# Split up projection with folded gain and bias, three of sixteen products on POOL, statistics moved

## The reference

```
xz = x @ w_in.T + b_in;  x_ssm, z = split(xz);  z = silu(z)
dt = softplus(x_ssm @ w_dt.T + b_dt);  Bm, Cm = x_ssm @ w_B.T + b_B, x_ssm @ w_C.T + b_C
per token:  h = exp(A * dt) * h + dt * Bm * x_ssm      (256 channels x 16 states)
            y = sum over the states of h * Cm
y = (y + D * x_ssm) * z;  x3 = layernorm(y @ w_out.T + b_out + x) * gamma + beta
h = layernorm(x3) * ln_gamma + ln_beta
out = layernorm(x3 + 0.5 * (silu(h @ w1 + fc1_bias) @ w2 + fc2_bias))
w1 = (fc1_q - 128) * fc1_scales,  w2 the same way;   w1 is 256 x 1024
```

## Time and profile before

| | |
|---|---|
| median of 3 runs (lowest, highest) | 1116.26 us (1113.83, 1117.23) |
| the profiled execution | 1115.44 us, of it the span 1113.7 us |
| mean granted TensorE clock | 0.968 |
| PE, DVE, ACT, POOL busy | 90%, 85%, 78%, 60% of the span |
| blocks 2 to 6, from first scan to first scan | 67.0 us each |

### The profile page before, as it was taken

The page is one execution under the profiler, slowest core; times in us unless marked ns, Lnnn a source line. Parts: engine busy times, 40 slices in busy tenths (PEclk is TensorE's granted clock), DMA queues, the critical chain, the costliest instruction groups (busy, mean ns, idle before and its releaser), DMA issues. The chain is left out here.

```text
span 1113.7 us, 17417 instructions
## 1 busy us (share of the span) xinstructions
PE 1006.3 (90%) x5326; PEld 716.2 (64%) x5326; DVE 950.2 (85%) x1237; ACT 864.7 (78%) x1688; POOL 666.4 (60%) x599
## 2 busy tenths in 40 slices
PE   5999999999969999997668799999999999988987
PEld 4777777777745555555345467676676756767576
DVE  7999999999955898675899999999999899999741
ACT  7778888787646677767858898898989989896833
POOL 3456566756760123135677968788696886968320
PEclk9999999999999999999869899999999999999999
DMA  6444434442405011125987555666457664755201
GB/s 188 127 131 120 133 104 135 119 135 89 128 20 191 1 38 39 38 77 150 213 168 159 130 152 123 169 135 171 134 152 156 150 157 133 158 138 133 75 1 38
DMA packets 93233, 133.84 MB, mean 120 GB/s; under 512 B 8787, under 2 KB 47699, under 8 KB 93141
## 3 DMA queue, kind: packets, MB, share of 16 engines
q1 hardware_dynamic: 93140, 132.73, 46.3%
HBM read 116.45 MB, written 14.16 MB: 117 GB/s over the span
## 5 line engine op out<-in xcount | busy, mean ns | idle before, releaser
L2265 DVE TENSOR_TENSOR_SCAN oa<-bank_a,h,oa 128x512 f32<-128x512 f32 x128 | 159.7, 1270 | 13.1 <-ACT h L1941 10.5
L2265 DVE TENSOR_TENSOR_SCAN ob<-bank_a,h,ob 128x512 f32<-128x512 f32 x128 | 160.4, 1269 | 9.5 <-ACT bank_a L1932 6.6
L1759 PE MATMUL bank_m<-w,f_h 128*128 128x256 f32 x448 | 104.6, 384 | 0.0
L40 PE MATMUL bank_m<-oa,w 128*128 128x512 f32 x224 | 102.9, 595 | 1.1 <-ACT oa L1999 0.9
L1932 ACT ACTIVATE bank_a<-dtc,A 128x512 f32<-128x512 f32 x128 | 86.7, 683 | 15.1 <-DVE ob L2265 7.6
L1932 ACT ACTIVATE bank_a<-s,A 128x512 f32<-128x512 f32 x128 | 86.5, 682 | 14.9 <-DVE oa L2265 8.8
L1472 POOL TENSOR_TENSOR oa<-ob,x1T 128x1024 f32<-128x1024 f32 x8 | 18.9, 2357 | 126.8 <-DVE ob L1374 126.8
L1759 PEld LDWEIGHTS bank_m<-w,f_h 128*128 128x128 f32 x448 | 84.8, 193 | 13.1 <-issue 2.4
L1714 PE MATMUL bank_y<-ident,ob 128*128 128x128 f32 x512 | 71.4, 286 | 20.2 <-DVE ob L2271 20.2
L1937 ACT ACTIVATE bank_c<-Cb 128x512 f32<-128x512 f32 x128 | 75.5, 590 | 16.9 <-DVE ob L2271 12.6
L2474 POOL TENSOR_TENSOR oa<-uc,Bb 128x1024 f32<-128x1024 f32 x32 | 75.7, 2365 | 21.4 <-DVE ob L2271 11.0
(11 more groups left out here) (386 smaller groups left out, 2787.1 us busy)
## 6 DMA issues: line engine op xcount, KB each, us to landing
Bb<-CB_rows SPq DMA_DIRECT2D x128, 256.0 KB, 4.9
Cb<-CB_rows SPq DMA_DIRECT2D x128, 256.0 KB, 4.7
abc<-decays SPq DMA_DIRECT2D x32, 512.0 KB, 4.4
Ebc<-ramps SPq DMA_DIRECT2D x64, 128.0 KB, 3.0
uT<-in_uT SPq DMA_DIRECT2D x8, 512.0 KB, 4.7
u<-in_u SPq DMA_DIRECT2D x8, 512.0 KB, 3.9
x_tokens<-x2s SPq DMA_DIRECT2D x8, 512.0 KB, 3.5
x_rows<-x1T SPq DMA_DIRECT2D x8, 512.0 KB, 2.9
```

Of the source, the lines that this page charges most:

```text
L40: i = e.matmul(out, w, x, start=(n == 0), stop=(n == len(pairs) - 1))
L1759: i = e.matmul(to, f_h[:, k, c * CH:(c + 1) * CH], w2[:, k, :], start=False, stop=(c % 2 == 1 and k == KF - 1))
L2265: e.tensor_tensor_scan(s[:, k, :], p_a[k][:, :], s[:, k, :], h0[:, n, k:k + 1], ALU.mult, ALU.add).then_inc(v_s, 1)
```

## The change

1. The up projection is split. w1, multiplied by ln_gamma, is kept as `w1_h` (rounded to float32r) and `w1_l` (the rest), and the normed input as `nT_h` and `nT_l`. `up_proj` does six float32r matmuls (h\*h, l\*h for each k, then h\*l) in place of two float32 ones. DVE makes `nT_l` in two new instructions `low` per block. ln_beta @ w1 is folded into the bias `b1s` ahead, so `evac_normed` becomes a plain copy. The weights for it are prepared in the coupling stage: 16 matmuls of one column (32 records) on PE at turn 8, two activations on ACT, and other instructions on DVE. `tw` has one buffer in place of two.
2. Products of states 0, 11 and 13 are made on POOL, straight from `Cb`, without `spread_C`. A second counter `p_g` counts them; `add_up`, `into` and `load_C` wait for it where such a product is concerned.
3. `stats6(old, 0)` moves next to `stats6(old, 1)`, after `product(cur, 1)` and `norm4(last, 0)` on ACT moves ahead of `decay(post, 13, 0)`. On POOL `into(cur, 5)` moves ahead of `shifted`.

```diff
+            p_g, on_pool = d_sem("p_g"), (0, 11, 13)
+            def pool_made(count):
+                return count // NS * len(on_pool) + sum(n < count % NS for n in on_pool)
+            def vector_made(count):
+                return count - pool_made(count)
                 def load_C(b, n):
-                    after(e, a_c, NS * b + n - 3)
+                    if n % NS >= 4 or b > 0:
+                        if (n - 4) % NS in on_pool:
+                            e.wait_ge(p_g, pool_made(NS * b + n - 3))
+                        else:
+                            e.wait_ge(a_c, vector_made(NS * b + n - 3))
                 def add_up(b, n):
-                    e.wait_ge(v_g, NS * b + n + 1)
+                    if n in on_pool:
+                        e.wait_ge(p_g, pool_made(NS * b + n + 1))
+                    else:
+                        e.wait_ge(v_g, vector_made(NS * b + n + 1))
                 def up_proj(b, m):
+                    if m < 2:
+                        e.wait_ge(v_nl, 2 * b + m + 1)
+                    else:
+                        e.wait_ge(a_up, 8 * b + m - 1)
                     if m == 0:
                         e.wait_ge(a_ft, 2 * b + 2)
-                    elif m > 1:
-                        e.wait_ge(a_up, 8 * b + m - 1)
-                    passes(e, pair[m % 2][:, :], [(w1[:, k, m * P:(m + 1) * P], nT[:, k, :]) for k in range(KD)]).then_inc(pe_up, 1)
+                    for k in range(KD):
+                        e.matmul(pair[m % 2][:, :], w1_h[:, k, ws], nT_h[:, k, :], start=(k == 0), stop=False)
+                        e.matmul(pair[m % 2][:, :], w1_l[:, k, ws], nT_h[:, k, :], start=False, stop=False)
+                    if m == 0:
+                        e.wait_ge(v_nl, 2 * b + 2)
+                    for k in range(KD):
+                        i = e.matmul(pair[m % 2][:, :], w1_h[:, k, ws], nT_l[:, k, :], start=False, stop=(k == KD - 1))
+                    i.then_inc(pe_up, 1)
 ...
+                    if w == 8:
+                        e.wait_ge(c_w, 3)
+                        for m in range(KF):
+                            i = passes(e, b_x[0][:, m:m + 1], [(s1[:, k, m * P:(m + 1) * P], lb[:, k:k + 1]) for k in range(KD)])
+                        i.then_inc(c_fold, 1)
 ...
+                def low(b, k):
+                    e.wait_ge(a_ft, 2 * b + k + 1)
+                    after(e, pe_up, 8 * b)
+                    e.tensor_tensor(nT_l[:, k, :], pair[k][:, :], nT_h[:, k, :].bitcast(F32), ALU.subtract).then_inc(v_nl, 1)
 ...
             def pool(e):
...
+                def product(b, n):
+                    e.wait_ge(v_s, 2 * (NS * b + n) + 2)
+                    e.wait_ge(ld_C[n % 4], DMAS * (4 * b + n // 4 + 1))
+                    after(e, pe_y, NS * b + n - 1)
+                    e.sem_inc(step, 1)
+                    e.tensor_tensor(prod[n % 2][:, :, :], state[(NS * b + n) % 4][:, :, :], both(Cb[n % 4][:, :]), ALU.mult).then_inc(p_g, 1)
```

More of the change, by code:

```diff
@@ L1068, in coupling @@
             loaded = [(x[:, :, :], y) for x, y in loaded]
-            loaded += [(w1[:, :, :].bitcast(I32), rows(d["f_q1"])), (w2[:, :, :].bitcast(I32), rows(d["f_q2"]))]
+            q1 = [flat(dtc[0]).bitcast(I32), flat(uc[0]).bitcast(I32)]
+            loaded += [(q1[k], rows(d["f_q1"])[:, k, :]) for k in range(KD)] + [(w2[:, :, :].bitcast(I32), rows(d["f_q2"]))]
             loaded += [(s1[:, k, :], d["f_s1"][k:k + 1, :].to_broadcast([P, FF])) for k in range(KD)]
@@ L1341, in scalar @@
                         evac_channels(ended(w - 5))
+                    if w in (13, 14):
+                        k = w - 13
+                        e.wait_ge(c_w, 3)
+                        e.activation(w1_h[:, k, :], s1[:, k, :], ACT.Copy, scale=lg[:, k:k + 1]).then_inc(c_wx, 1)
                     if w == 19:
@@ L2036, in end_normed @@
                     e.wait_ge(pe_ft, 2 * Z + p + 1)
-                    for k in range(KD):
-                        e.activation(nT[:, k, p * DM:(p + 1) * DM], wide[p][:, k * DM:(k + 1) * DM], ACT.Identity, bias=lb[:, k:k + 1], scale=lg[:, k:k + 1]).then_inc(a_ft, 1)
+                    e.activation(nT_h[:, :, p * DM:(p + 1) * DM], wide[p][:, :].rearrange("p (k t) -> p k t", k=KD), ACT.Copy).then_inc(a_ft, 1)
                 def end_norm4(p):
@@ L2060, in scalar @@
                 decay(0, 0, 1)
-                spread_C(0, 0)
                 c_evac(NB - 2)
@@ L2100, in scalar @@
                     if live(post):
-                        spread_C(post, 11)
                         decay(post, 12, 0)
@@ L2108, in scalar @@
                         carry(post, 11)
+                    if 0 <= last < NB - 1:
+                        norm4(last, 0)
+                    if live(post):
                         decay(post, 13, 0)
@@ L2114, in scalar @@
                         evac_up(last, 1)
-                        norm4(last, 0)
                     if live(post):
@@ L2120, in scalar @@
                         evac_up(last, 2)
-                    if live(post):
-                        spread_C(post, 13)
                     if 0 <= last < NB - 1:
@@ L2155, in scalar @@
                         c_normalize(NB - 1, 1)
-                    if 0 < cur < NB:
-                        spread_C(cur, 0)
                     if 0 <= last < NB - 1:
@@ L2384, in vector @@
                         scan(post, 10, 0)
-                    if 0 <= old < NB - 2:
-                        stats6(old, 0)
                     if live(post):
@@ L2390, in vector @@
                         scan(post, 11, 0)
+                    if 0 <= last < NB - 1:
+                        low(last, 0)
+                    if live(post):
                         product(post, 10)
+                    if 0 <= last < NB - 1:
+                        low(last, 1)
+                    if live(post):
                         scan(post, 11, 1)
-                    if live(post):
-                        product(post, 11)
                         scan(post, 12, 0)
@@ L2401, in vector @@
                         scan(post, 14, 1)
-                        product(post, 13)
                         scan(post, 15, 0)
@@ L2414, in vector @@
                     if live(cur):
-                        product(cur, 0)
                         scan(cur, 1, 1)
@@ L2423, in vector @@
                     if 0 <= old < NB - 2:
+                        stats6(old, 0)
                         stats6(old, 1)
@@ L2460, in vector @@
                 second(Y, 1)
+                end_low(0)
                 stats6(Y, 1)
+                end_low(1)
                 end_second(0)
@@ L2582, in pool @@
                         into(cur, 0)
+                    if live(post):
+                        product(post, 13)
+                    if 0 < cur < NB:
                         into(cur, 1)
@@ L2586, in pool @@
                         into(cur, 3)
+                        product(cur, 0)
                         into(cur, 4)
+                    if live(cur):
+                        into(cur, 5)
                     if 0 <= post < NB - 1:
@@ L2591, in pool @@
                         norm6(old)
-                    if live(cur):
-                        into(cur, 5)
                     if 0 <= post < NB - 1:
@@ L2618, in pool @@
                         into(cur, 14)
+                        product(cur, 11)
                         into(cur, 15)
```

77 lines of the change are left out of this document (50 added, 27 removed).

## The result

| | before | after |
|---|---|---|
| median of 4 runs, us (lowest, highest) | 1116.19 (1113.83, 1117.23) | **1147.52** (1145.52, 1153.10) |
| ratio, 95% interval | | **1.0291** (1.0269 to 1.0312) |
| profiled execution, its span | 1115.44, 1113.7 | 1145.52, 1143.6 |
| mean granted TensorE clock | 0.968 | 0.944 |

The change costs 31 us; the forecast was +25 and 1141 us, the range 1118 to 1157. The median lies just above the band of 1135 to 1147 us that the prediction gave its own case.

A forecast was written before the change was run, and what follows sets the result against it. DVE and PE, each busy 63.7 of 66.9 us a block, left little room, and lateness on PE lengthens the block. Six stalls +25.8, block 0 -1, coupling stage +3.5, end section -2.6: 1115.4 + 25.7 = 1141.1 us; range 1118 to 1157.

The forecast's parts named there:

- its own case: Whole kernel: the forecast itself, 1135 to 1147 us, given a 50% chance.
- The place of product 11: POOL's list, behind into 14: PE would wait 4.9 us at add_up(11), in six blocks, iterations 2 to 7.
- The work behind it: PE after the wait: five add_up and seven up_proj, 14.75 us to the end of add_up(15); +2.6 us per block.
- The clock: PE behind the wait: 3.4 us at half clock, +1.7 us per block, bounds 0 and 3.4.
- rival "twice as long": PE's clock low for twice as long, +10.2 us, or the load landing in 4.9 us: 1148 to 1158 us; 14%.
- Product 13: POOL, behind into(cur, 0): ready before PE needs it, wait taken as 0, with 1.2 us kept in the range.
- DVE's wait behind the stall: DVE behind ACT's late second evac_up: idle for about 2 us.
- The coupling stage: PE at turn 8: 32 one-column records at 0.112 us each, +3.5 us; other weight instructions 0, with 2 either side.
- Block 0: First block, without an up projection: one product less ahead of its silu, -1 us.
- The end section: 16 tiles of 256 columns at 0.68 instead of 0.87 us, +0.4 for waiting for end_low: -2.6 us.
- Iteration 8: Same order there, but PE arrives late against POOL after a 2.96 us wait, so no stall: 0 us.
- The faster rival: DVE is the bound and gets its relief, -2.7 us in each of 7 blocks: 1097 us; 12%.

The follow-up runs named there:

- e1: Changed kernel with product 11 back on DVE and its spread_C back on ACT, products 0 and 13 still on POOL: 1119.55 us.
- e7: Changed kernel with only POOL's list edited, product 11 ahead of into 14 and product 13 directly behind into 15: 1125.66 us.
- e6: Changed kernel with only PE's list edited, up_proj 1, 2 and 3 ahead of add_up(11): 1143.13 us.
- e8: e7 plus up_proj 1 and 2 ahead of add_up(11), 3 behind it; on ACT evac_up(1) ahead of decay(14, 0), norm4(0) behind that: 1105.50 us.
- e5: Changed kernel with 18 extra float32r matmuls on PE ahead of add_up(11), to keep it busy in the wait: 1137.60 us.
- e3: Kernel before with the three products on POOL at the places of the change and nothing else: 1156.29 us.
- e4: Changed kernel without the 32 one-column records at turn 8, so the ln_beta part of the bias is missing: 1143.55 us.
- e2: Changed kernel with all three products back on DVE and their spread_C back; split up projection and moved statistics stay: 1123.19 us.
- e10: Kernel before with the three products on POOL and the POOL, PE and ACT orders of e8, without split or moved statistics: 1111.39 us.
- e11: e8 with stats6(old, 0) back at its old place behind scan(10, 0): 1108.03 us.

## Why the prediction was right, and where it was off

The mechanism was right. The profiled execution is 4.4 us above the 1141.1 of the sum: +3.2 in the coupling stage, +1.6 in block 0, +0.9 in the end section, -1.1 in block 7 and -0.3 in blocks 1 to 6. That the six blocks agree to 0.3 us is in part luck: 4.3 each were forecast, and they grew by 4.9, 3.0, and from 4.1 to 4.6.

**The place of product 11.** Said: PE ready at 52.9 us of the block, product over at 57.9, a wait of 4.9. Measured in block 4: PE free at 52.7, product over at 57.5, 4.82. The prediction took six equal stalls; they were 3.3 us in block 1 and 4.8 in the five others. Taking the product off POOL (e1), moving it up POOL's list (e7), and moving the `add_up` down PE's (e6, e8) all moved the time in the direction and by nearly the amount the queue says.

**The work behind it.** 14.75 + 1.7 = 16.45 us to the end of `add_up(15)` were forecast. PE took 16.35 (857.91 to 874.26). `up_proj` is 1.40 to 1.49 us a tile, the `low` on DVE 0.6 from start to start.

**The clock.** 1.7 us a block was taken from one wait of before. The low clock lasted 6.8 us, twice as long as assumed, but 2.1 of them lay in the wait, and e5 measured a loss of 1.7 to 1.9 by the blocks. How long it lasts seems to count, which was not tried by itself: in e3, with waits of 4.3 us throughout, blocks 3 and 5 have 6.8 us of it and take 73.8 and 73.9 us, blocks 4 and 6 have 3.4 and take 72.7. The rival "twice as long" had the length right and the price wrong. The rule cited from the Trainium skill ("TensorE: Matmul & The Clock Gate", section "HAM oscillation — how this bites in real kernels"), that a wait between bursts makes each iteration start slow, agrees with this trace: the clock is at 0.50 behind the wait in block 4, and at 1.00 there where the wait was filled (e5).

**Product 13.** Taken as hidden, with a wait of 1.2 us left in the range. In block 4 it ended at 868.4, and PE came to it at 868.92: hidden by half a microsecond, behind a load for which POOL waited 3.2 us. Both stood later in the block than forecast, 68.1 and 68.6 us and not 65.8 and 66.8, for the low clock was in neither sum. Where the clock stays up (e5) the load of B sets the end: PE came to the product 0.05 us after it was over in block 4, and waited 1.15 us in block 6, where the load took 4.8 us to land and not 3.7. So the 0 that was taken was a near thing; e6 shows the wait in full.

**DVE's wait behind the stall** was put at 2 us and was 3.7 and 1.7. The block came out at the forecast all the same (71.4 us, forecast 71.3). Not all of it came by the path that was named, though: against before, `z_proj(1)` stands 3.9 us later in block 4, the load of silu's table 4.1, and the block is 4.4 longer. The last half microsecond lies behind `z_proj`, where the prediction kept the old distances, and no run took it apart.

**The coupling stage is the term that was off: "+3.5".** It measured +6.7 up to scan 0. The records alone took 3.6 (393.89 to 397.49), as said. What failed is that nothing was taken for the clock behind them: e4 puts the whole at 4.6. Another 0.8 is drift of the first stage, whose code is the same. The remaining 1.3 are left for the other weight instructions, inside the 2 allowed; they were not tried by themselves.

**Block 0**, "-1", was +0.6. The prediction looked for the wait only behind an up projection, but PE waits 4.96 us for product 11 in block 0 too, and with POOL's order changed (e7) the block is 3.0 us shorter. Its DMA share is 0.84, and in e4 it was 64.9: that it gives back to the loads what comes ahead of it fits, and was not tried by itself. **The end section**, "-2.6", was -1.7: a tile of 256 columns takes 0.71 us (0.68 expected), and PE waits 0.60 us for the first `end_low` alone. That the term is the split's is not shown: with the split alone (e2) the end section is 0.6 shorter than before, with product 11 on DVE (e1) 0.7 longer. **Iteration 8**, "0", was -1.1: a wait of 1.40 us in place of 4.8, so nearly no stall, as argued. The 1.1 are not shown to be DVE's relief, since with all products on DVE (e2) block 7 takes 65.2 us, nearly the same as with the change (64.9).

**The faster rival** (DVE's relief, 12%) was not empty. The gain is there: with both orders changed the blocks are 1.8 us shorter than before. About 0.5 of that comes with the products (e10), 0.8 with the split and 0.6 with the moved statistic (e11). It had been conditional on POOL reaching product 11 in time "or an `add_up` elsewhere in PE's list", and it needed both.

## What to carry to other kernels

Work moved to an engine that is idle "on average" must be placed by the time at which its consumer stands in another queue, not by the time at which its input is ready: here the product stood behind one `into` of 2.3 us, while another engine's list had seven tiles behind it. Moving it ahead of that one instruction, with product 13 moved up too, was the step from 1147.5 to 1125.7 us (one run for the two moves together). An engine that takes over one such instruction needs its neighbours' lists changed with it, since a wait that was filled in one place (e6) turned up at two others, 2.3 us at `evac_up(1)` and 1.3 to 3.8 us at the next product. When a wait of TensorE is priced, add what the clock costs behind it, and look in the stage's other waits for a home for new small matmuls.

## What the runs showed of the hardware

The granted clock fell without a wait. Behind the 32 one-column records, PE was busy in the whole stretch, and yet the clock was 0.50 from 398.4 to 401.8. The same happens in all eight kernels that have the records there. What in them does it was not tried. The first fence is the changed kernel: the records, the stretch behind them, and the one after that. The second is the kernel without the records, at 1.00 there though PE has 0.8 us of idle time in it.

```profile
393.90:397.50 3.60, 3.60 (x35) 3.60 (x33) 3.47 (x4) 0.95 (x3) 0.00 (x0) 1.00 0.00 0
398.40:401.80 3.40, 3.40 (x10) 2.37 (x8) 1.21 (x3) 0.69 (x1) 2.02 (x1) 0.50 0.00 0
401.80:405.20 3.40, 3.40 (x17) 1.70 (x16) 1.92 (x9) 2.10 (x4) 0.34 (x1) 1.00 0.00 0
```

```profile
398.40:401.80 3.40, 2.57 (x11) 1.34 (x10) 3.35 (x9) 1.36 (x3) 3.13 (x3) 1.00 0.00 0
```

A product of 128x1024 float32 from SBUF took 2.35 us on POOL and 1.20 on DVE, with one operand in PSUM there. The Trainium skill ("GPSIMD Engine Reference", section "3.1 Elementwise — side-by-side cycle accounting") puts POOL at about half of VectorE's speed for an elementwise float32 instruction with two inputs; the trace agrees, with 1.96.
